# First half of x in four tile transfers, and the gates on a semaphore of their own

## The chip, the cores and the metric

The kernel runs on 1 core of a Trainium2 chip. The metric is the device time of one execution in microseconds (us); smaller is better. Its engines are TensorE (PE, with its weight loads as PEld), VectorE (DVE), ScalarE (ACT), GpSimd (POOL) and SyncE (SP), which here only issues the transfers.

## The reference, cut to what matters

x is 4 x 256 tokens of 256 channels, ctx_2048 has the same shape. Four residual steps follow each other, each gated by the tanh of one of four scalars:

```python
x = x + tanh(g_xattn[0]) * wkv(w, u, layernorm(x), ctx_2048)       # a scan over 256 tokens
x = x + tanh(g_ffn[0])   * ternary_ffn(layernorm(x), ...)          # inner size 1024
x = x + tanh(g_xattn[1]) * cross_attention(layernorm(x), ctx_2048) # 32 heads of 8
x = x + tanh(g_ffn[1])   * experts(layernorm(x), ...)              # 64 experts, top 8, and a shared one
```

In `wkv` the keys are the normed x and the values are ctx_2048; the running maximum of the keys, two decayed sums and their quotient are computed token by token in each channel.

## The kernel before

The 1024 tokens lie in x as 8 tiles of 128 tokens (TT = 8); a half is 4 tiles (HT = 4). Every engine has one stream of instructions, written out by hand, and waits on semaphores; a transfer adds 16 to its semaphore when it has landed.

SP issues all transfers. At the start it issues, with no wait between them: x, tiles 0 to 3 (`ld_x[0]`); identf, wkv, gates and identh (all on `ld_const`, which so reaches 64); ctxT (1 MB, `ld_ctx`); three blocks of FFN weights (1 MB each, `ld_ffn`); proj and gate (`ld_proj`); x, tiles 4 to 7 (`ld_x[1]`). Its first wait is for the splits of the context and the projections into halves, ahead of the expert weights.

DVE starts with `constants()`, `stats(0)` (bn_stats of tiles 0 to 3 at L1009, aggregation at L1012, then `ve`), `signs()` (the negated gates and wkv), `norm(0)` (the root's correction, then xn at L1028), `low_part(0)` (the low part of ctxT, L1287), and the scans: `running_max(0)`, `running_max(1)` (L1049, L1051), `sums_a`, `sums_b` and so on to the quotients (L1096).

ACT starts with `gains()` (tanh of the gates, L749), `table_exp_ln()` (a table load, L752), `norm_root(0)` (Ln at L564, Exp at L566), `high_context()` (the high part of ctxT, L763), `keys_before_steps(0)` (the turned keys out of PSUM, L682), `abs_sum(0)` (the first FFN block, L578), and the exponentials of the scans.

PE turns the normed tiles (L1554, `turn_norm(0)`), and next projects the context (L1562) once the projections are split.

`stats(q)` is called for 12 groups of tiles, 32 tiles in all (`NORM_TILES`); each call waits once, on the semaphore of its half:

```python
NORM_TILES = [(0, 4), (0, 4), (0, 2), (4, 8), (2, 4), (0, 2), (4, 8), (2, 4), (4, 6), (6, 8), (4, 6), (6, 8)]
```

Behind that come the FFN and attention of the first half (to about 165 us), and then 65 passes over pairs of experts (L1562 and L1892 on PE), with the second half's attention worked in among them.

Of the kernel before, what the change touches and what calls it, by code (L numbers as in the profile page):

```python
# [18 lines left out]
TT = NT // P  # L19
HT = TT // 2  # L20
# [26 lines left out]
def bass_flamingo(nc, x_in, ctxT_in, wkv_in, g_in, ffn_in, proj_in, gate_in, gu_in, dp_in,  # L47
                  identf_in, identh_in, routing, out):
    with ExitStack() as stack:
        def sb(name, shape, dt=F32):  # L50
            return stack.enter_context(nc.sbuf_tensor(name, shape, dt))

        def sem(name):
            return stack.enter_context(nc.semaphore(name))
# [4 lines left out]
        x = sb("x", [P, TT, D])  # L59
# [4 lines left out]
        gates = sb("gates", [P, 4])  # L64
# [110 lines left out]
        def bank(i, n=1):  # L175
            return ps[:, 512 * i:512 * (i + n)]


        ld_x = [sem(f"ld_x{i}") for i in range(2)]
        ld_const = sem("ld_const")  # L180
        ld_ctx = sem("ld_ctx")
        ld_proj = sem("ld_proj")
        ld_ffn = [sem(f"ld_ffn{i}") for i in range(3)]
# [85 lines left out]
        x_rows = x_in.rearrange("(t p) d -> p t d", p=P)  # L269
# [27 lines left out]
        def normed_rows(q):  # L297

            return sum(b - a for i, (a, b) in enumerate(NORM_TILES[:q]) if i not in FFN_NORMS)

        def halves_before(q):
            return DK * SPLIT_NORMS.index(q)
# [178 lines left out]

        @block.sync
        def _(sp):
            sp.dma_start(x[:, 0:HT, :], x_rows[:, 0:HT, :]).then_inc(ld_x[0], 16)
            sp.dma_start(identf[:, :], identf_in).then_inc(ld_const, 16)
            sp.dma_start(wkv[:, :, :], wkv_in).then_inc(ld_const, 16)
            sp.dma_start(gates[:, :], g_in).then_inc(ld_const, 16)
            sp.dma_start(identh[:, :], identh_in).then_inc(ld_const, 16)
            sp.dma_start(ctxT[:, :, :], ctxT_in).then_inc(ld_ctx, 16)
            for i in range(3):  # L490
                sp.dma_start(fst[i], ffn_in[:, i, :]).then_inc(ld_ffn[i], 16)
            sp.dma_start(proj[:, :, :], proj_in).then_inc(ld_proj, 16)
            sp.dma_start(gate[:, :, :], gate_in).then_inc(ld_proj, 16)
            sp.dma_start(x[:, HT:TT, :], x_rows[:, HT:TT, :]).then_inc(ld_x[1], 16)

            def load_entry(e):
                if e >= NS:
                    sp.wait_ge(mwH_ready, e - NS + 1)
                    sp.wait_ge(mwL_ready, e - NS + 1)
                p = ENTRY_PAIR[e]  # L500
                if p == SHARED:
                    to = mst[:, e % NS, 0:2 * DK * P].rearrange("p (b n) -> p b n", n=P)
                    of = gu_in[:, p, :].rearrange("p (b n) -> p b n", n=P)[:, :, 0:EI]
                    for i in range(2):
                        rows = slice(i * EI, (i + 1) * EI)
                        sp.dma_start(to[:, :, rows], of).then_inc(ld_pair[e % NS], 16)
                        sp.dma_start(mst[rows, e % NS, 2 * DK * P:PW], dp_in[0:EI, p, :]).then_inc(ld_pair[e % NS], 16)
                    return
                sp.dma_start(mst[:, e % NS, 0:2 * DK * P], gu_in[:, p, :]).then_inc(ld_pair[e % NS], 16)
                sp.dma_start(mst[:, e % NS, 2 * DK * P:PW], dp_in[:, p, :]).then_inc(ld_pair[e % NS], 16)  # L510

            def store_routing(h):
                sp.wait_ge(WT_ready, h + 1)
                sp.dma_start(routing[:, h * HALF:(h + 1) * HALF], WT[0:E + 1, :]).then_inc(WT_stored, 16)
                sp.wait_ge(WT_stored, 16 * (h + 1))

            def store_out(h):
                sp.wait_ge(out_ready, HT * (h + 1))
                sp.dma_start(out_rows[:, HT * h:HT * (h + 1), :], x[:, HT * h:HT * (h + 1), :]).then_inc(out_done, 16)


            sp.wait_ge(splitH, 3)
            sp.wait_ge(splitL, 3)
            for e in range(NS + EARLY):
                load_entry(e)
            store_routing(0)
            sp.wait_ge(y_turned, TT)
            for c in range(NCH):
                p, h = CHUNKS[c]
                if c in LOAD_IN:  # L530
                    load_entry(LOAD_IN[c])
                if c == SHARED - 1:
                    store_routing(1)
                if c == FIRST_DONE + 9:
                    store_out(0)
                if c >= NR:
                    sp.wait_ge(inter_ready, c - NR + 1)
                for i in range(2):
                    row, half = (E, i) if p == SHARED else (2 * p + i, h)
                    sp.dma_start(route[i * EI:(i + 1) * EI, c % NR, :],  # L540
                                 routing[row:row + 1, half * HALF:(half + 1) * HALF].broadcast_to([EI, HALF])
                                 ).then_inc(ld_route[c % NR], 16)
            store_out(1)
            sp.wait_ge(out_done, 32)

        @block.scalar
        def _(act):
# [197 lines left out]
                                     scale=ROUTING_SCALE).then_inc(WT_ready, 1)  # L745

            def gains():
                act.wait_ge(ld_const, 64)
                nc.scalar.activation(tg[:, :], gates[:, :], ACT.Tanh).then_inc(tanh_done, 1)  # L749

            def table_exp_ln():
# [13 lines left out]
            def high_projections():  # L765
                act.wait_ge(ld_proj, 32)
                nc.scalar.activation(projH[:, :, :], proj[:, :, :], ACT.Copy, scale=W_SCALE).then_inc(splitH, 1)
                nc.scalar.activation(gateH[:, :, :], gate[:, :, :], ACT.Copy, scale=W_SCALE).then_inc(splitH, 1)

            gains()  # L770
            table_exp_ln()
            norm_root(0)
# [184 lines left out]
        def _(dve):  # L957
            done = [0]

            def post(ins):  # L960
                done[0] += 1
                ins.then_inc(v_ord, 1)

            def settle():
                dve.wait_ge(v_ord, done[0])
# [8 lines left out]
            def root_begin(src, n, mul, eps):  # L974
                e = begun[0]
                begun[0] += 1
                V.tensor_scalar(ve[:, e % 2, 0:n], src, mul, eps, ALU.mult, ALU.add).then_inc(var_ready, 1)
# [26 lines left out]
            def stats(q):  # L1004

                a, b = NORM_TILES[q]
                dve.wait_ge(ld_x[a // HT], 16)
                for t in range(a, b):
                    post(V.bn_stats(bn[:, t, :], x[:, t, :]))  # L1009
                settle()  # L1010
                for t in range(a, b):
                    post(V.bn_aggr(mv[:, t, :], bn[:, t, :]))  # L1012
                settle()
                if q < BITS_FROM:
                    root_begin(mv[:, a:b, 1], b - a, 1.0, LN_EPS)
# [286 lines left out]
            def signs():  # L1302
                dve.wait_ge(tanh_done, 1)
                post(V.tensor_scalar(ntg[:, :], tg[:, :], -1.0, None, ALU.mult))
                post(V.tensor_scalar(tgd[:, :], tg[:, 3:4], DOWN_UNSCALE, None, ALU.mult))
                dve.wait_ge(ld_const, 64)
                V.tensor_scalar(nwkv[:, :, :], wkv[:, :, :], -1.0, None, ALU.mult).then_inc(wkv_negated, 1)

            constants()
            stats(0)  # L1310
            signs()
            norm(0)
# [14 lines left out]
            row_sums(0)  # L1327
            add_y(0, 4)
            stats(1)
            ternary_weights(0)  # L1330
            norm(1)
# [8 lines left out]
            ffn_residual(1, 6)  # L1340
            row_sums(1)
            stats(2)
            rows_begin(0)
            norm(2)
# [181 lines left out]
        def _(pe):  # L1526
# [3 lines left out]
            def take(b, sem_value):  # L1530

                if b in reader:
                    pe.wait_ge(*reader[b])
                reader[b] = sem_value

            def turn_norm(q, b0):

                a, b = NORM_TILES[q]
                if q == 0:
                    pe.wait_ge(ld_const, 64)  # L1540
                for k in range(DK):
                    if q in FFN_NORMS:
                        take(b0 + k, (xq_ready, DK * FFN_NORMS.index(q) + k + 1))
                    elif q in STEP_NORMS:
                        take(b0 + k, (kT_ready, DK * STEP_NORMS.index(q) + k + 1))
                    else:
                        take(b0 + k, (hL_ready, halves_before(q) + k + 1))
                for t in range(a, b):
                    if q in FFN_NORMS:
                        pe.wait_ge(xz_ready, t + 1)  # L1550
                    else:
                        pe.wait_ge(xn_ready, normed_rows(q) + t - a + 1)
                    for k in range(DK):
                        mm = T.transpose(bank(b0 + k)[:, (t - a) * P:(t - a + 1) * P], xn[:, t, k * P:(k + 1) * P], identf[:, :])  # L1554
                mm.then_inc(xn_turned, 1)
# [419 lines left out]
```

## Time and profile before

| | before |
|---|---|
| runs | 495.12, 496.13, 498.81 us; median 496.13 |
| profiled execution, its own time | 494.66 us |
| its span | 492.9 us |
| busy PE, DVE, ACT | 401.6 (81%), 384.4 (78%), 305.9 us (62%) |
| mean granted TensorE clock | 0.946 of full speed |
| DMA | 47.47 MB, mean 96 GB/s |

The span is the profiler's, from the first instruction to the last; the device time of the same execution is 1.76 us longer. A busy share is an average over stages with different limits, so that the place of the change, the first 13 us, has to be read from views of that stretch. "SPq" is the issue of a transfer on SP; the data moves later, by the DMA engines.

### The profile page before, as it was taken

The page shows a single profiled execution, that of the slowest core. Times are in us where ns is not written, and L with a number is a line of the kernel's source. Part 1 is how long each engine was busy: PE and PEld are TensorE (multiplying, and loading weights), DVE is VectorE, ACT ScalarE, POOL GpSimd, SP SyncE. Part 2 cuts the span into 40 slices and gives each one's busy share as a digit, 9 for nine tenths or more (in the row PEclk, how much of TensorE's full clock was granted, in tenths as well). Part 3 has the DMA queues.
Part 4 walks back from the last instruction along what each step waited for, and adds up shares of the span by engine and source line. Part 5 has one row for each costly group of instructions (what it writes and reads, how often), then busy time and mean ns, then how long its engine had stood idle before and what let it go on. Part 6 is the DMA issues. An engine that isn't in the chain of part 4 may idle for free.

```text
span 492.9 us, 7899 instructions
## 1 busy us (share of the span) xinstructions
PE 401.6 (81%) x2606; PEld 191.7 (39%) x2606; DVE 384.4 (78%) x867; ACT 305.9 (62%) x473; POOL 0.2 (0%) x4
## 2 busy tenths in 40 slices
PE   1041765777774999989999899899999999999994
PEld 1020353332332555444334433444444444444442
DVE  5999489898999789999878876886546776677744
ACT  5989576689893785648887678463233445544431
POOL 0000000000000000000000000000000000000000
PEclk9996889595998799999999999999999999999999
DMA  8420000000020151525246332234421755555501
GB/s 306 198 65 1 0 1 1 1 1 2 1 65 4 47 165 57 158 88 168 67 118 191 98 108 72 91 108 125 132 65 54 217 164 164 164 177 172 171 22 43
DMA packets 31491, 47.47 MB, mean 96 GB/s; under 512 B 5594, under 2 KB 15194, under 8 KB 30940
## 3 DMA queue, kind: packets, MB, share of 16 engines
q1 hardware_dynamic: 31452, 46.98, 30.4%
q8 instruction: 21, 0.34, 0.3%
q14 instruction: 18, 0.15, 0.1%
HBM read 45.65 MB, written 1.31 MB: 95 GB/s over the span
## 4 chain that ended last, share of the span: by engine, by line
PE 47%; DVE 30%; ACT 8%; issue 7%; DMA 5%; SPq 2%; DVEq 0%; ACTq 0%
PE ps L1562 25%; PE ps L1892 12%; PE ps L1667 4%; DMA regP<-in_dp_dram 4%; PE ps L1655 2%; DVE regW L1277 2%; DVE bn L1009 1%; DVE tiny L1194 1%; ACT regO L584 1%; DVE xn L1028 1%; DVE regW L1481 1%; DVE regW L1472 1%; PE ps L1583 1%; DVE rep L1155 1%; DMA regC<-in_ctxT_dram 1%
## 5 line engine op out<-in xcount | busy, mean ns | idle before, releaser
L1562 PE MATMUL ps<-hH,regC 128*128 128x512 f16 x264 | 85.5, 379 | 1.1 <-ACT regW L934 0.9
L1481 DVE TENSOR_TENSOR regW<-ps,regW 128x512 f32<-128x512 f32 x65 | 44.9, 690 | 52.6 <-PE ps L1562 50.1
L934 ACT ACTIVATE regW<-ps 128x512 f32<-128x512 f32 x52 | 31.0, 596 | 86.6 <-PE ps L1562 83.5
L1562 PE MATMUL ps<-hH,regW 128*128 128x512 f16 x248 | 81.8, 386 | 1.4 <-ACT regW L934 0.8
L1562 PE MATMUL ps<-hL,regC 128*128 128x512 f16 x132 | 50.0, 379 | 0.0
L1892 PE MATMUL ps<-regW,regC 128*128 128x512 f16 x198 | 48.2, 379 | 0.5 <-DVE regW L1472 0.5
L1562 PE MATMUL ps<-hL,regW 128*128 128x512 f16 x124 | 47.8, 385 | 0.0
L1892 PE MATMUL ps<-regW 128*128 128x512 f16 x186 | 45.3, 380 | 0.7 <-DVE regW L1472 0.7
L1472 DVE TENSOR_TENSOR regW<-regW 128x512 f16<-128x512 f32 x65 | 44.4, 682 | 1.0 <-ACT regW L941 0.7
L941 ACT CAST regW<-regW 128x512 f16<-128x512 f32 x65 | 39.8, 612 | 6.4 <-DVE regW L1494 6.1
L1562 PEld LDWEIGHTS ps<-hH,regC 128*128 128x128 f16 x264 | 25.8, 98 | 33.3 <-issue 2.6
L723 ACT ACTIVATE exs<-ps 128x1024 f32<-128x1024 f32 x32 | 32.0, 1023 | 9.4 <-PE ps L1655 8.6
L1562 PEld LDWEIGHTS ps<-hH,regW 128*128 128x128 f16 x248 | 24.5, 99 | 33.0 <-issue 3.9
L1494 DVE TENSOR_TENSOR regW<-regW 128x512 f32<-128x512 f32 x52 | 35.6, 685 | 0.1
L723 ACT ACTIVATE regF<-ps 128x1024 f32<-128x1024 f32 x32 | 32.0, 1026 | 5.0 <-PE ps L1667 2.2
L732 ACT ACTIVATE regC<-regP 128x768 f16<-128x768 f32 x30 | 25.3, 844 | 15.7 <-DMA regP<-in_dp_dram 15.7
L1277 DVE SCALAR_TENSOR_TENSOR regC<-regP,regC 128x768 f16<-128x768 f32 x30 | 28.5, 953 | 8.1 <-ACT regC L732 8.0
L1554 PE MATMUL ps<-identf,xn 128*128 128x128 f32 x64 | 12.6, 341 | 26.4 <-DVE xn L1028 15.8
L1655 PE MATMUL ps<-regO,KT 32*128 32x256 f16 x256 | 21.8, 290 | 9.4 <-ACT exs L723 3.8
L1892 PEld LDWEIGHTS ps<-regW,regC 128*128 128x128 f16 x198 | 19.1, 98 | 24.1 <-DVE regW L1472 1.0
L732 ACT ACTIVATE regW<-regP 128x768 f16<-128x768 f32 x27 | 22.6, 844 | 8.8 <-DMA regP<-in_dp_dram 8.5
L1277 DVE SCALAR_TENSOR_TENSOR regW<-regP,regW 128x768 f16<-128x768 f32 x27 | 25.5, 952 | 2.9 <-ACT regW L732 2.9
(189 smaller groups left out, 657.1 us busy)
## 6 DMA issues: line engine op xcount, KB each, us to landing
regW<-routing_dram SPq DMA_DIRECT2D x130, 128.0 KB, 3.1
regP<-in_gu_dram SPq DMA_DIRECT2D x56, 256.0 KB, 2.7
regP<-in_dp_dram SPq DMA_DIRECT2D x56, 128.0 KB, 2.8
regO<-in_ffn_dram SPq DMA_DIRECT2D x3, 1024.0 KB, 9.0
x<-in_x_dram SPq DMA_DIRECT2D x2, 512.0 KB, 8.2
regC<-in_ctxT_dram SPq DMA_DIRECT2D x1, 1024.0 KB, 5.0
out_dram<-x SPq DMA_DIRECT2D x2, 512.0 KB, 3.3
regP<-in_proj_dram SPq DMA_DIRECT2D x1, 768.0 KB, 12.1
```

What stands on the lines that cost most here:

```text
L723: nc.scalar.activation(Ex[u % NE], bank(b0, 2).rearrange("p (j n) -> p j n", j=2), ACT.Exp, scale=float(HD) ** -0.5).then_inc(prob_ready, 1)
L732: nc.scalar.activation(mwH[e % NW], mst[:, e % NS, :], ACT.Copy, scale=W_SCALE).then_inc(mwH_ready, 1)
L934: nc.scalar.activation(sgm[:, c % 2, :], bank(gate_bank(c)), ACT.Silu, scale=UNSCALE).then_inc(esilu_done, 1)
L941: nc.scalar.copy(inH[:, d % 2, :], inter[:, d % 2, :]).then_inc(inH_ready, 1)
L1277: V.scalar_tensor_tensor(mwL[e % NW], mst[:, e % NS, :], W_SCALE, mwH[e % NW], ALU.mult, ALU.subtract).then_inc(mwL_ready, 1)
L1472: V.tensor_tensor(inL[:, d % 2, :], inter[:, d % 2, :], inH[:, d % 2, :], ALU.subtract).then_inc(inL_ready, 1)
L1481: V.tensor_tensor(rows, bank(gate_bank(c) + 1), rows, ALU.mult).then_inc(et_done, 1)
L1494: V.tensor_tensor(rows, route[:, c % NR, :], sgm[:, c % 2, :], ALU.mult).then_inc(inter_ready, 1)
L1562: mm = T.matmul(out_ap, w(k), a(k), start=(n == 0), stop=(n == 3 * DK - 1))
L1655: mm = T.matmul(bank(b0 + jj)[:, mt * S:(mt + 1) * S], KT[r:r + 32, g, b * S + mt * P:b * S + (mt + 1) * P], QT[r:r + 32, g, (b % 2) * S:( ...
L1667: mm = T.matmul(bank(bk)[32 * j:32 * j + HD + 1, 0:S], vaug[:, 2 * b + mt, 4 * g + j, :], Ex[u % NE][:, j % 2, mt * S:(mt + 1) * S], start ...
L1892: mm = T.matmul(bank(ACC[h] + k), w[s][:, at], a[:, c % 2, :], start=(c == 0 and n == 0), stop=(c == NCH - 1 and n == 2), skip_group_check ...
```

## The change

The first half of x is loaded by four transfers of one tile each, each on a semaphore of its own; the second half takes the fifth. The gates are loaded between the first and the second tile, on `ld_gates`. ScalarE's tanh waits for `ld_gates` alone; the others wait for the three transfers left on `ld_const` (48 in place of 64). DVE's `stats` waits ahead of each tile, not once ahead of a group.

```diff
-        ld_x = [sem(f"ld_x{i}") for i in range(2)]
+        ld_x = [sem(f"ld_x{i}") for i in range(HT + 1)]
         ld_const = sem("ld_const")
+        ld_gates = sem("ld_gates")
@@ SP
-            sp.dma_start(x[:, 0:HT, :], x_rows[:, 0:HT, :]).then_inc(ld_x[0], 16)
+            for t in range(HT):
+                sp.dma_start(x[:, t, :], x_rows[:, t, :]).then_inc(ld_x[t], 16)
+                if t == 0:
+                    sp.dma_start(gates[:, :], g_in).then_inc(ld_gates, 16)
             sp.dma_start(identf[:, :], identf_in).then_inc(ld_const, 16)
             sp.dma_start(wkv[:, :, :], wkv_in).then_inc(ld_const, 16)
-            sp.dma_start(gates[:, :], g_in).then_inc(ld_const, 16)
             sp.dma_start(identh[:, :], identh_in).then_inc(ld_const, 16)
             sp.dma_start(ctxT[:, :, :], ctxT_in).then_inc(ld_ctx, 16)
@@
-            sp.dma_start(x[:, HT:TT, :], x_rows[:, HT:TT, :]).then_inc(ld_x[1], 16)
+            sp.dma_start(x[:, HT:TT, :], x_rows[:, HT:TT, :]).then_inc(ld_x[HT], 16)
@@ ACT gains()
-                act.wait_ge(ld_const, 64)
+                act.wait_ge(ld_gates, 16)
                 nc.scalar.activation(tg[:, :], gates[:, :], ACT.Tanh).then_inc(tanh_done, 1)
@@ DVE stats(q)
-                dve.wait_ge(ld_x[a // HT], 16)
                 for t in range(a, b):
+                    dve.wait_ge(ld_x[min(t, HT)], 16)
                     post(V.bn_stats(bn[:, t, :], x[:, t, :]))
@@ DVE signs()
-                dve.wait_ge(ld_const, 64)
+                dve.wait_ge(ld_const, 48)
@@ PE turn_norm(0)
-                    pe.wait_ge(ld_const, 64)
+                    pe.wait_ge(ld_const, 48)
```

## Rows read from the trace of the kernel before

**Rows 1.** The page's chain that ended last, its shares by engine.
```profile
PE 47%; DVE 30%; ACT 8%; issue 7%; DMA 5%; SPq 2%; DVEq 0%; ACTq 0%
```

**Rows 2.** That chain in order of time, 0 to 40 us: start, length, what.
```profile
3.18 4.96 DMA regC<-in_ctxT_dram
...
10.22 0.05 issue
```

**Rows 3.** Timeline of ACT, 0 to 16 us: start, length, operation, idle before and its releaser.
```profile
5.12 0.21 ACT L749 ACTIVATE tg<-gates 128x4 f32<-128x4 f32 x1 [3.12 <-DMA identh<-in_identh_dram]
5.35 1.28 ACT L752 ACT_TABLE_LOAD   x1
6.64 0.20 ACT L564 ACTIVATE lnv<-ve 128x4 f32<-128x4 f32 x1
...
8.25 1.91 ACT L763 ACTIVATE ctxH<-regC 128x2048 f16<-128x2048 f32 x1 [1.17 <-DMA regC<-in_ctxT_dram]
10.52 1.07 ACT L682 COPY regC<-ps 128x512 f32<-128x512 f32 x2 [0.36 <-PE ps L1554]
11.48 1.92 ACT L578 ACTIVATE regF<-regO 128x2048 f32<-128x2048 f32 x1
```

**Rows 4.** Timeline of DVE, 0 to 40 us.
```profile
4.32 1.41 DVE L1009 BATCH_NORM_STATS2 bn<-x 128x6 f32<-128x256 f32 x4 [2.58 <-DMA x<-in_x_dram]
...
6.18 0.17 DVE L977 TENSOR_SCALAR ve<-mv 128x4 f32<-128x4 f32 x1
...
7.99 1.38 DVE L1028 TENSOR_SCALAR xn<-x,mv,rstd 128x256 f32<-128x256 f32 x4
10.27 2.29 DVE L1287 SCALAR_TENSOR_TENSOR ctxL<-regC,ctxH 128x2048 f16<-128x2048 f32 x1 [0.90 <-ACT ctxH L763]
12.48 1.27 DVE L1049 TENSOR_TENSOR_SCAN regW<-wkv,regC 128x256 f32<-128x256 f32 x2
...
36.73 1.66 DVE L1178 SCALAR_TENSOR_TENSOR x<-ps,ntg,x 128x256 f32<-128x256 f32 x4
```

**Rows 5.** Timeline of SP's queue, 0 to 8 us: start and length of each issue.
```profile
0.73 0.43 SPq L484 DMA_DIRECT2D x<-in_x_dram  x1
1.22 0.49 SPq L485 DMA_DIRECT2D identf<-in_identf_dram  x1
...
2.23 0.43 SPq L487 DMA_DIRECT2D gates<-in_g_dram  x1
2.70 0.43 SPq L488 DMA_DIRECT2D identh<-in_identh_dram  x1
3.18 0.43 SPq L489 DMA_DIRECT2D regC<-in_ctxT_dram  x1
```

**Rows 6.** Stretches of 0.25 us: clock, DMA share and GB/s stand last.
```profile
4.40:4.65 0.25, 0.00 (x0) 0.00 (x0) 0.25 (x1) 0.00 (x0) 0.00 (x0) 1.00 0.00 0
...
5.40:5.65 0.25, 0.00 (x0) 0.00 (x0) 0.25 (x2) 0.25 (x1) 0.00 (x0) 1.00 1.09 459
```

**Rows 7.** DMA issues of 0 to 40 us: count, KB each, median us to landing.
```profile
identf<-in_identf_dram SPq DMA_DIRECT2D x1, 64.0 KB, 3.1
identh<-in_identh_dram SPq DMA_DIRECT2D x1, 32.0 KB, 2.4
...
gates<-in_g_dram SPq DMA_DIRECT2D x1, 2.0 KB, 2.5
```

**Rows 8.** Line L484 alone: time from issue to landing.
```profile
DMA to landing us min/median/max: 3.6/3.6/3.6
```

**Rows 9.** Line L491 alone, the three FFN blocks.
```profile
DMA to landing us min/median/max: 7.0/9.0/11.0
```

**Rows 10.** Line L1178 alone: durations of one in ns.
```profile
L1178 DVE SCALAR_TENSOR_TENSOR x<-ps,ntg,x x8: 474/476/485, 36.7 to 131.8; 128x256 f32<-128x256 f32 x8
```

**Rows 11.** Longer stretches: length, busy PE, PEld, DVE, ACT, POOL, granted clock, DMA.
```profile
82.60:96.30 13.70, 8.42 (x69) 4.58 (x70) 12.72 (x37) 7.52 (x13) 0.00 (x0) 0.57 0.01 1
...
110.00:120.10 10.10, 5.75 (x52) 1.60 (x56) 9.50 (x21) 9.66 (x18) 0.00 (x0) 0.60 0.00 1
120.20:154.20 34.00, 23.70 (x292) 12.52 (x284) 31.83 (x92) 26.48 (x40) 0.00 (x0) 0.97 0.08 25
...
164.50:488.70 324.20, 313.50 (x1860) 144.64 (x1858) 242.64 (x498) 184.07 (x284) 0.00 (x0) 1.00 0.39 119
```

## The prediction

> **What bounds the kernel now.** I read the page's chain first. It ends on PE (47%) and passes through DVE (30%) [rows 1], and from 164.5 to 488.7 us PE is busy 313.50 of 324.20 us at the full granted clock [rows 11]: the passes over the experts are bound by PE. The change doesn't touch that part; it can only make it begin sooner or later. So the question is what sets the start of the work, and the chain in order of time answers it: at the front of the chain stands not x, but the load of ctxT, issued at 3.18 us and landed 4.96 us later, at 8.14 [rows 2]. I then read each engine's timeline over the first 16 us, to see both paths that meet at the first scan.
>
> The path of x: the first half lands 3.6 us after its issue at 0.73 [rows 5, 8], bn_stats starts at 4.32 and `ve` at 6.18 [rows 4]. ACT has its tanh only at 5.12, after 3.12 us of idleness that identh's landing ended, and the table load behind it runs from 5.35 to 6.63; so Ln starts at 6.64, 0.29 us after `ve` is finished at 6.35 [rows 3, 4]. The normed tiles start at 7.99 and are done at 9.37 [rows 4].
>
> The path of ctxT: ACT is idle 1.17 us until it lands, makes ctxH from 8.25 to 10.16, and DVE, idle for 0.90 us, makes ctxL from 10.27 to 12.56; the first scan starts at 12.48 [rows 3, 4]. In DVE's stream ctxL stands ahead of the scan, and in ACT's stream ctxH stands ahead of the copy of the keys. The copy runs from 10.52 to 11.59 [rows 3], so the keys are there 0.89 us before DVE is free to scan. Of the two paths the one of ctxT ends last, twice: once at ACT (the idle 1.17 us) and once at DVE (the idle 0.90 us). What the change hastens is the other one.
>
> **Part by part.**
>
> *The three additional transfers.* SP issues five transfers ahead of ctxT, at 0.73, 1.22, ... and 2.70, and ctxT itself at 3.18: (3.18 - 0.73) / 5 = 0.49 us from one to the next [rows 5]. With the change eight stand ahead of it: four of x, gates, identf, wkv, identh. It is issued 3 x 0.49 = 1.47 us later, at 4.65. What lies beside this: nothing on SP, whose queue has no wait here.
>
> Does a later issue make a later landing? Only if the DMA engines aren't still busy with what lies ahead. From 4.40 to 4.65 us they moved nothing at all, 0 GB/s, and from 5.40 they move 459 GB/s [rows 6]. The queues had run dry before ctxT's data began, so its landing follows from its issue. I take the whole 1.47 us: landing at 4.65 + 4.96 = 9.61. The bounds are 0, if ctxT's own transfer goes faster in its new place, and 3 x (2.23 - 1.22) / 2 = 1.52 us at the widest spacing shown [rows 5]; a case below 0 is excluded, since no transfer is taken from in front of ctxT.
>
> *The Trainium skill on this cost.* The rows put 0.43 us of SP's time and 0.49 us of spacing on one issue. "DMA: Bandwidth & Descriptors", section "Anatomy of one DMA — SWDGE (gpsimd) path", puts about 50 ns on the sequencer's dispatch and calls descriptor generation small. By that page three more issues would be an estimated 0.15 us, and the sum would be 0.15 in place of 1.47. The page describes transfers issued by GpSimd and these are SP's; this trace doesn't agree with the page's figure.
>
> *The tiles of x.* Their issues come at 0.73, 1.70, 2.19 and 2.68 us (gates at 1.22). No load of 128 KB stands alone at the start; a 64 KB one landed 3.1 us after its issue, a 32 KB one 2.4 and a 2 KB one 2.5 [rows 7], and four tiles at once took 3.6 [rows 8]. So a tile takes between 2.4 and 3.6; I take 2.6, near the small ones, as its data is a quarter of x's. Tile 0 is there at about 3.3 and tile 3 at 5.3 (5.1 to 6.3). Before, all four were there at about 4.3. Three of the bn_stats run earlier under the loads, the fourth starts at about 5.3 and is done at 5.7, which is where the last of the four ended before, 4.32 + 1.41 = 5.73 [rows 4]. So the stats of the half gain nothing: `ve` stays at about 6.2, with 6.0 to 7.1 as its bounds.
>
> *The gates.* They land at 1.22 + 2.5 = 3.7 [rows 7]; tanh and its following table load are done at about 3.7 + 0.05 + 0.21 + 0.02 + 1.28 = 5.3, in place of 6.63 [rows 3]. Then Ln waits for `ve` alone and starts at about 6.4, a gain of 0.25 us. The xn tiles end at about 9.1 in place of 9.37. All of this ends at ACT's wait for ctxT, which now lasts until 9.61: worth nothing.
>
> *identf, wkv and identh.* identf and wkv move back by four places (1.96 us), identh by three (1.47 us), since gates used to stand between wkv and identh. identh, the last of the three, is issued at 4.17 and lands 2.4 us later [rows 7], at about 6.6. DVE's `signs()` waits for it, and queued behind that wait are `norm(0)` and all that follows; but `norm(0)` needs ACT's root, which comes at about 6.9. The cover is 0.3 us. PE waits for the same semaphore, and needs xn until about 7.7 anyway. If identh is late by more than the cover, the xn path moves, and it has room: xn may end 1 us late before the copy of the keys waits.
>
> *What is then late next.* ctxH runs from 9.72 to 11.63, ctxL from 11.74 to 14.03, and the first scan starts at about 13.95 in place of 12.48. The copy of the keys stands behind ctxH in ACT's stream; before, it waited 0.36 us for PE's last turn [rows 3], now PE has long finished, and it runs from about 11.65 to 12.75, still ahead of the scan. Then the first FFN block: it lands 7.0 us after its issue at the soonest of the three [rows 9], about 10.7 before and 12.1 after, and `abs_sum(0)` took it at 11.48 [rows 3] and will at 12.65. Cover 0.5 us, and behind it another idle stretch until the first exponential. The other blocks, proj, gate and the second half of x have many microseconds.
>
> *The additional waits in stats.* 12 waits become 32, 20 more. Whether a wait for a semaphore long reached costs DVE anything, I read from the residual sum at L1178, which also waits ahead of each tile: four took 1.66 us [rows 4] and one 0.476 [rows 10], so that (1.66 - 0.476) / 3 = 0.395 us lie between starts, less than one lasts. The wait is hidden behind the running instruction. Bounds: 0 and 20 x 0.05 = 1.0 us, with 0.05 as a typical gap of the chain [rows 2]; I take 0.
>
> *How far the shift gets.* From the first scan on DVE, ACT and PE hand work to each other, and no transfer of the start is awaited that has less than the cover named above. A uniform shift of all three engines then reaches the expert passes whole, and the end with them. The one thing tied to time and activity rather than to semaphores is TensorE's clock. In 82.6 to 96.3 and in 110.0 to 120.1 us the granted clock averaged 0.57 and 0.60 [rows 11], nearly at the 1.2 GHz level of its two. If the edges of these stretches move against the work, the sum changes by a share of a microsecond per edge.
>
> **The sum.** +1.47 (ctxT's issue), 0 (stats), 0 (tanh), 0 (waits) = +1.47 us. Against the profiled execution's own time this is 494.66 + 1.5 = 496.1. That execution was 1.5 us below the median of the runs, so on the median it is 496.13 + 1.47 = 497.6 us, 0.3% slower. No change of this kernel under 1% can be told from none by its measurement, whose three runs span 0.7%.
>
> **The rivals.**
>
> *The landing doesn't follow the issue, or slack swallows the shift (not slower).* If what sets ctxT's landing is the bytes queued ahead of it, which the change leaves equal, it lands at 8.14 still. For it: the DMA engines run near full share from 5.4 us. Against it: the stretch with 0 GB/s just before [rows 6]. Or the first scan has slack further on. Then the xn path, 0.25 us earlier, still ends behind ctxH, and the time is 496.1 us, at best 0.25 less.
>
> *The clock turns against it (slower).* If moving the work by 1.5 us puts one more stretch of 10.2 us at half clock into 120 to 154 us, where PE is busy 23.70 of 34.00 us [rows 11], up to 0.70 x 10.2 / 2 = 3.6 us are lost: 497.6 + 3.6 = 501.2. It decides from the point where PE is on the chain in that stretch. For it: such stretches exist on both sides of it. Against it: the pattern of work is the same, only moved.
>
> *The clock turns in its favour.* One such stretch less, of 110.0 to 120.1, with 5.75 us of PE, gives back at most 2.9 us [rows 11]: 494.7.
>
> *The additional waits cost what they can.* 497.6 + 1.0 = 498.6.
>
> **How the numbers follow.** The forecast has 0.60 (496.9 to 498.2), no shift 0.15, the clock against it 0.10, half of it over the 1% bound, the clock in its favour 0.08, the waits 0.07. The predicted time is 497.6. The range goes down to 495.0, past no shift at all and into the favourable clock, and up to 500.3, past the waits and into the unfavourable clock. Over 1% faster would take a second stretch of clock in its favour, 0.03; over 1% slower 0.05; within 1% 0.92.
>
> **What would show it.** SP's queue: ctxT issued at 4.65. ACT: tanh at about 3.8, then Ln at 6.4, then an idle time of about 2.7 us ended by ctxT's landing. DVE: the last bn_stats at 5.3, ctxL at 11.7, the first scan at 13.9. The expert passes begin 1.5 us later. I am wrong if ctxT lands as early as before, if the first scan starts before 13, or if the delay at 13 us is no longer there at 165.

## The result, and the profile after

| | before | changed |
|---|---|---|
| median of 20 runs | 495.54 us | 498.23 us |
| lowest, highest | 494.04, 498.81 | 495.50, 500.99 |
| profiled execution, its own time | 494.66 | 499.49 |
| its span | 492.9 | 497.6 |

The ratio is 1.0038 with a 95% interval from 1.0021 to 1.0055: slower by 1.9 us (1.0 to 2.7), below the 1% that counts as no change. 1.47 us had been forecast, and 498.23 lies inside the range of 495.0 to 500.3.

The timeline of SP's queue in the changed kernel (start, length, what was issued):

```profile
0.73 0.38 SPq L486 DMA_DIRECT2D x<-in_x_dram  x1
1.17 0.42 SPq L488 DMA_DIRECT2D gates<-in_g_dram  x1
1.64 1.38 SPq L486 DMA_DIRECT2D x<-in_x_dram  x3
3.06 0.43 SPq L489 DMA_DIRECT2D identf<-in_identf_dram  x1
...
4.48 0.43 SPq L492 DMA_DIRECT2D regC<-in_ctxT_dram  x1
```

It answers to [rows 5]. ctxT is issued at 4.48 in place of 3.18, 1.30 us later for three issues more. 1.47 had been worked out from 0.49 us an issue; here the eight ahead of ctxT follow each other by 0.47 us on average, (4.48 - 0.73) / 8. ACT's timeline, to be held against [rows 3]:

```profile
3.04 0.20 ACT L752 ACTIVATE tg<-gates 128x4 f32<-128x4 f32 x1 [1.04 <-DMA gates<-in_g_dram]
3.27 1.28 ACT L755 ACT_TABLE_LOAD   x1
6.08 0.20 ACT L567 ACTIVATE lnv<-ve 128x4 f32<-128x4 f32 x1 [1.52 <-DVE ve L980]
...
9.61 1.91 ACT L766 ACTIVATE ctxH<-regC 128x2048 f16<-128x2048 f32 x1 [3.10 <-DMA regC<-in_ctxT_dram]
11.43 1.05 ACT L685 COPY regC<-ps 128x512 f32<-128x512 f32 x2
```

The reader should see two things. What the change set out to hasten is earlier: tanh at 3.04 and not 5.12, Ln at 6.08 and not 6.64. And all of it ends in an idle time that grew from 1.17 to 3.10 us: ACT stands and waits for ctxT. DVE shows the same, to be held against [rows 4]:

```profile
2.88 0.43 DVE L1012 BATCH_NORM_STATS2 bn<-x 128x6 f32<-128x256 f32 x1 [1.14 <-DMA x<-in_x_dram]
4.09 1.33 DVE L1012 BATCH_NORM_STATS2 bn<-x 128x6 f32<-128x256 f32 x3 [0.79 <-DMA x<-in_x_dram]
...
7.42 1.38 DVE L1031 TENSOR_SCALAR xn<-x,mv,rstd 128x256 f32<-128x256 f32 x4
11.63 2.29 DVE L1290 SCALAR_TENSOR_TENSOR ctxL<-regC,ctxH 128x2048 f16<-128x2048 f32 x1 [2.83 <-ACT ctxH L766]
13.84 1.27 DVE L1052 TENSOR_TENSOR_SCAN regW<-wkv,regC 128x256 f32<-128x256 f32 x2
```

The normed tiles start 0.57 us earlier (7.42 for 7.99), ctxL and the first scan 1.36 us later (13.84 for 12.48). The two profiled executions, however, differ by 4.8 us, not 1.4. The rest comes behind the scans. The chain in order of time, changed kernel first, then the kernel before (start, length, what):

```profile
30.12 1.77 DVE projL L1290
...
31.93 5.28 PE ps L1565 x12
37.24 0.38 ACT kc L632
```

```profile
35.22 0.69 DVE regC L1096
...
36.35 6.06 ACT regO L584 x3
```

In the changed kernel's execution the 12 matmuls of the first projections are themselves on the chain; in the one of before they were not. So one of the experiments, e9, is the question how far two executions of the same program differ.

### The profile page after: what moved, and what is told of

The parts are those of the page before. It is cut to its first block, busy times and chain, and to the rows that moved or that the text cites. A ratio compares the mean times of both kernels' runs of the same rounds, so it can differ in the third digit from the quotient of the medians.

```text
span 497.6 us, 7902 instructions
## 1 busy us (share of the span) xinstructions
PE 404.6 (81%) x2606; PEld 193.4 (39%) x2606; DVE 384.9 (77%) x867; ACT 305.9 (61%) x473; POOL 0.2 (0%) x4
## 4 chain that ended last, share of the span: by engine, by line
PE 49%; DVE 30%; ACT 7%; issue 7%; DMA 4%; SPq 2%; DVEq 0%; ACTq 0%
PE ps L1565 26%; PE ps L1895 12%; PE ps L1670 4%; DMA regP<-in_dp_dram 3%; DVE tiny L1197 2%; PE ps L1658 2%; DVE regW L1280 2%; DVE bn L1012 2%; DVE xn L1031 1%; ACT regO L587 1%; DVE regW L1484 1%; DVE regW L1475 1%; DVE regF L1209 1%; PE ps L1586 1%; DMA regC<-in_ctxT_dram 1%
```

## The experiments

My theory: ctxT's landing sets the first scan, it follows from its issue, each issue ahead of it costs 0.47 to 0.49 us, and the shift reaches the end whole; split, waits and gates cost and give nothing. Rivals: the split of x or the 20 waits cost by themselves; slack swallows the shift; the landing goes by the bytes ahead; the difference is the clock's. Every ratio is to runs of the kernel before on the same chip. The columns "x through" and "ctxT begins" come from the list of packets in the trace: x's first half travels in 512 packets of 1 KB, ctxT and the FFN blocks in packets of 8 KB. They give the end of x's last packet and the start of the first 8 KB packet; "to landing" is the time from ctxT's issue to its landing.

| kernel | ctxT issued | x through | ctxT begins | to landing | first scan | ratio, 95% interval |
|---|---|---|---|---|---|---|
| before | 3.18 | 3.87 | 4.23 | 5.0 | 12.48 |  |
| e9, before again | 3.19 | 3.84 | 4.26 | 5.5 | 12.99 | 1.0019 (0.9998 to 1.0040) |
| changed | 4.48 | 4.64 | 5.55 | 5.0 | 13.84 | 1.0038 (1.0021 to 1.0055) |
| e11, changed again | 4.48 | 4.49 | 5.55 | 5.1 | 13.89 | 1.0039 (1.0015 to 1.0063) |
| e1, three issues more | 4.61 | 3.70 | 5.68 | 5.3 | 14.23 | 1.0011 (0.9991 to 1.0032) |
| e4, nine issues more | 7.46 | 3.69 | 8.53 | 5.0 | 16.75 | 1.0087 (1.0061 to 1.0114) |
| e5, waits alone | 3.19 | 3.75 | 4.25 | 5.3 | 12.82 | 1.0013 (0.9988 to 1.0038) |
| e6, gates alone | 3.19 | 3.80 | 4.27 | 5.6 | 13.17 | 1.0019 (0.9991 to 1.0046) |
| e2, ctxT sixth, small ones behind | 3.06 | 4.68 | 4.15 | 7.0 | 15.04 | 1.0015 (0.9996 to 1.0034) |
| e3, ctxT third, small ones behind | 1.77 | 3.93 | 3.77 | 7.6 | 14.40 | 1.0019 (0.9998 to 1.0039) |
| e7, small ones by ACT, ctxT third | 1.78 | 4.90 | 3.98 | 7.3 | 13.38 | 1.0012 (0.9985 to 1.0039) |
| e8, small ones by ACT, ctxT sixth | 3.06 | 5.07 | 4.42 | 7.5 | 14.94 | 1.0053 (1.0028 to 1.0077) |
| e10, identh last | 2.72 | 3.76 | 3.85 | 5.6 | 12.65 | 0.9977 (0.9952 to 1.0002) |
| e12, identh last, gates second | 2.71 | 3.88 | 4.41 | 5.4 | 12.50 | 1.0006 (0.9979 to 1.0033) |

**e1, e4: the issues without the split.** The kernel before with 3 or 9 transfers of 2 KB into a spare tile ahead of ctxT:

```diff
             sp.dma_start(identh[:, :], identh_in).then_inc(ld_const, 16)
+            for i in range(3):      # 9 in e4
+                sp.dma_start(spare[:, i, :], g_in).then_inc(ld_spare, 16)
             sp.dma_start(ctxT[:, :, :], ctxT_in).then_inc(ld_ctx, 16)
```

> The kernel before with three additional 2 KB transfers between identh and ctxT; x whole, the gates and all waits as they were. If the cost of the change is the three additional issues ahead of ctxT: ctxT issued at about 4.5 to 4.6 us, landed at about 9.5, first scan at about 13.8, time 1.4 us above before plus whatever the clock does (ratio 1.003, within 1.001 to 1.0055). If the cost lies in the split of x or in the additional waits on DVE: first scan at 13.8 all the same, but a time equal to before (ratio 1.000), or the landing stays at 8.1 if only bytes count.

> As the first of these, with nine additional 2 KB transfers: the suspected cost three times over. If a shift of the first scan reaches the end whole: ctxT issued at 3.2 + 9 x 0.47 = 7.4, first scan at 16.7, time 4.2 us above before (ratio 1.0085, 1.006 to 1.011). If the difference of the change is the clock's (more half-clock stretches after any disturbance of the start, whatever its size): ratio 1.003 to 1.005 here as well. If slack swallows a part: under 1.006.

SP's queue in e4, then DVE's timeline in e4:

```profile
3.19 4.23 SPq L492 DMA_DIRECT2D spare<-in_g_dram  x9
7.46 0.43 SPq L493 DMA_DIRECT2D regC<-in_ctxT_dram  x1
```

```profile
16.75 1.27 DVE L1054 TENSOR_TENSOR_SCAN regW<-wkv,regC 128x256 f32<-128x256 f32 x2
```

Nine issues take 4.23 us, 0.47 each; ctxT lands 5.0 us after its issue, and the scan is 4.27 us late. The time, from six runs, is 0.87% longer, 4.3 us (3.0 to 5.7). Within that interval the shift reaches the end whole, and it isn't a fixed toll of the clock. e1 repeats the changed kernel's place of ctxT (issued at 4.61) with x in one piece and moves the scan by 1.75 us; its ratio of 1.0011 holds 0 as well as 1.6 us and decides nothing on the time.

**e5, e6: the other parts alone.** e5 has only the waits ahead of each tile, e6 only the gates, second in the queue with their own semaphore; the tanh waits for that one, and the other waits on `ld_const` go from 64 to 48.

```diff
-                dve.wait_ge(ld_x[a // HT], 16)
                 for t in range(a, b):
+                    dve.wait_ge(ld_x[t // HT], 16)      # e5
```

```diff
             sp.dma_start(x[:, 0:HT, :], x_rows[:, 0:HT, :]).then_inc(ld_x[0], 16)
+            sp.dma_start(gates[:, :], g_in).then_inc(ld_gates, 16)      # e6; removed from ld_const
```

> The kernel before with nothing but the waits of the change: stats waits ahead of each tile, on the semaphore of its half, 20 waits more. If satisfied waits are free: every group of four bn_stats lasts 1.41 us as before, first scan at 12.5, ratio 1.000 (0.998 to 1.002). If each costs a gap of 0.05 us on the path: groups of 1.56 us, 1.0 us more in all, ratio 1.002.

> The kernel before with nothing but the gates' part of the change: second in the queue and on a semaphore of their own; x in one transfer, ctxT sixth as before. If only ctxT's landing counts: tanh about 0.5 to 1 us earlier, Ln at 6.4, ctxT landed at 8.1 and scan at 12.5, ratio 1.000. If the tanh and its table load were on the path: scan at 12.2, ratio 0.9995; the time can't tell these two apart, the trace can.

The second group of bn_stats in e5, all of whose waits are long satisfied (DVE's timeline):

```profile
38.76 1.41 DVE L1009 BATCH_NORM_STATS2 bn<-x 128x6 f32<-128x256 f32 x4
```

1.41 us for four, as without the waits [rows 4]. The satisfied waits cost nothing here. ACT's timeline of e6:

```profile
4.48 0.20 ACT L750 ACTIVATE tg<-gates 128x4 f32<-128x4 f32 x1 [2.47 <-DMA gates<-in_g_dram]
...
6.35 0.20 ACT L565 ACTIVATE lnv<-ve 128x4 f32<-128x4 f32 x1 [0.37 <-DVE ve L978]
...
8.94 1.91 ACT L764 ACTIVATE ctxH<-regC 128x2048 f16<-128x2048 f32 x1 [2.15 <-DMA regC<-in_ctxT_dram]
```

The tanh is 0.64 us earlier, Ln 0.29, and ACT then waits 2.15 us for ctxT: worth nothing, as with the tiles. ctxT itself landed 5.6 us after its issue at 3.19, where I had expected 5.0.

**e2, e3: giving ctxT its place back, or a better one.** e2 is the changed kernel, e3 the kernel before with the gates second; in both, identf, wkv and identh move behind ctxT.

```diff
+            sp.dma_start(ctxT[:, :, :], ctxT_in).then_inc(ld_ctx, 16)
             sp.dma_start(identf[:, :], identf_in).then_inc(ld_const, 16)
             sp.dma_start(wkv[:, :, :], wkv_in).then_inc(ld_const, 16)
             sp.dma_start(identh[:, :], identh_in).then_inc(ld_const, 16)
-            sp.dma_start(ctxT[:, :, :], ctxT_in).then_inc(ld_ctx, 16)
```

> The changed kernel with ctxT moved ahead of identf, wkv and identh, so that it is the sixth issue as before the change; four tile transfers, gates on their own semaphore and all waits kept. If only ctxT's issue counts: issued at about 3.1, landed at 8.1, ctxH at 8.2, scan at 12.4 to 12.5, ratio to before 1.000 (0.999 to 1.001). Rival: identf and identh now land behind 1 MB of context, near 8.2 or later, DVE's wait for identh holds norm(0) back and the normed path takes over as the last; the scan then comes at 12.5 to 13.5 and up to 1 us of the cost stays. If the split or the waits cost by themselves, the ratio stays at 1.003 with the scan at 12.5.

> The kernel before with x in one transfer, then the gates (own semaphore), then ctxT third, then identf, wkv, identh. If issue order sets the start: ctxT issued at 1.7 instead of 3.2, but its data now stands directly behind the 512 KB of x, so landing at about 6.7; ctxH at about 7.0, and DVE's norm(0), which waits for identh behind 1 MB of context until about 7, becomes the last: xn 8 to 9.4, ctxL from 9.4, scan at 11.6. Time 0.8 us below before (ratio 0.9985, 0.997 to 1.000). If the start is not on the path of the end, ratio 1.000.

Both missed. The landings (DMA issues of the first 15 us: count, KB, us to landing) and DVE's timeline of e3:

```profile
regC<-in_ctxT_dram SPq DMA_DIRECT2D x1, 1024.0 KB, 7.6
...
identf<-in_identf_dram SPq DMA_DIRECT2D x1, 64.0 KB, 5.6
identh<-in_identh_dram SPq DMA_DIRECT2D x1, 32.0 KB, 6.8
```

```profile
10.02 0.17 DVE L1308 TENSOR_SCALAR nwkv<-wkv 128x4 f32<-128x4 f32 x1 [3.53 <-DMA identh<-in_identh_dram]
...
12.20 2.28 DVE L1288 SCALAR_TENSOR_TENSOR ctxL<-regC,ctxH 128x2048 f16<-128x2048 f32 x1
...
14.40 1.27 DVE L1050 TENSOR_TENSOR_SCAN regW<-wkv,regC 128x256 f32<-128x256 f32 x2
```

ctxT, issued 1.41 us earlier than before, landed 1.2 us later, after 7.6 us in place of 5.0. And identh landed at 10, so that DVE, which waits for it ahead of `norm(0)`, lost the normed path too (3.53 us idle): ctxL starts at 12.20 with no idle time before it, behind the normed tiles. So here the normed path comes last, and in e2 as well (ctxL at 12.84, with no idle time before it either). It is the rival that e2's expectation names, with a larger effect than it allowed. These two kernels therefore don't isolate the split of x, as I had meant them to.

**e7, e8: the small ones out of SP's queue.** ScalarE issues identf, wkv and identh before its first table load; e8 is otherwise the changed kernel, e7 the kernel of e6.

```diff
+            for to, of in ((identf[:, :], identf_in), (wkv[:, :, :], wkv_in), (identh[:, :], identh_in)):
+                act.dma_start(to, of).then_inc(ld_const, 16)
             gains()
```

> As the one before, and identf, wkv and identh are issued by ScalarE's queue, so that SP issues x, gates, ctxT and then the FFN blocks. ctxT is issued at 1.7. If ctxT's landing follows its issue with 5.0 us wherever large blocks stand behind it: landed at about 6.8, scan limited by the normed path and ctxL behind it, at 11.5 to 11.8, time 0.8 us below before (ratio 0.9985). If small transfers in flight beside a large one stretch it, whichever queue they come from (as when they stood behind it on SP's queue, 7.0 and 7.6 us instead of 5.0): landed at 9 or later, scan at 13.5 or later, ratio over 1.002.

> The changed kernel, four tiles and gates first, with identf, wkv and identh issued by ScalarE's queue, so that ctxT is SP's sixth issue as before the change. If the cost of the change is ctxT's place alone: ctxT issued at 3.1, landed at 8.1, scan at 12.4, ratio 1.000. If the split of x costs by itself: ratio 1.003 with that scan. If small transfers beside it stretch it: landing at 9 or later.

Landing of ctxT in e8, and e8's stretches from the start of ctxT's data to its landing (length, busy times, clock, DMA share, GB/s):

```profile
regC<-in_ctxT_dram SPq DMA_DIRECT2D x1, 1024.0 KB, 7.5
...
identh<-in_identh_dram ACTq DMA_DIRECT2D x1, 32.0 KB, 3.2
```

```profile
4.40:10.50 6.10, 1.94 (x8) 1.57 (x8) 3.93 (x19) 1.00 (x3) 0.00 (x0) 1.00 0.96 341
```

and the kernel before over the corresponding stretch:

```profile
4.40:8.10 3.70, 0.00 (x0) 0.00 (x0) 2.85 (x17) 1.90 (x4) 0.00 (x0) 1.00 0.86 341
```

Small loads in flight beside ctxT can't be the cause in e8: there they have landed at 1.65 + 3.2 = 4.85 us, when ctxT's data has hardly begun. The rate is the same 341 GB/s. But in e8 6.10 x 341 = 2.08 MB passed before ctxT (1.05 MB) was complete, 1.98 MB of them in 8 KB packets, in the kernel before 3.70 x 341 = 1.26 MB. So about 0.7 MB more of the FFN blocks, which were issued later, had moved ahead of ctxT's last part. In e2 and e3 it is another picture: 269 GB/s from 4.20 to 10.10 us and 294 GB/s from 3.80 to 9.40 us, 1.6 MB each, with the packets of identf, wkv and identh among them. e8 is the slowest of the kernels with ctxT in sixth place, with the scan at 14.94 and a ratio of 1.0053: the landing counts, not the issue. e7 landed at 9.1 and its scan came at 13.38, near the second branch of what was expected; its ratio of 1.0012 was under it.

What the four slow landings have in common stands in the table. In the ten executions with 5.0 to 5.6 us x is through before ctxT begins, by 0.09 us (e10) to 4.84 us (e4). In the four with 7.0 to 7.6 us ctxT begins while packets of x are still under way, by 0.16 us (e3) to 0.92 us (e7). This is a regularity in 14 traces, not a shown cause: no experiment changed it alone, and all four also have small loads behind ctxT or on ScalarE's queue.

**e9, e11: the same two kernels again.** No edit.

> The kernel before, unchanged, as a control for the small ratios. Ratio 1.000 (0.998 to 1.002). Its profile is a second look at the start of that kernel: if the start of the first look was typical, ctxT lands at 8.1 to 8.5 and the first scan starts at 12.5 to 12.9. The places of the half-clock stretches should differ between the two looks although the program is the same.

> The changed kernel again, on the same chip as the control. If its cost is ctxT's place in the queue alone: scan at 13.8, ratio 1.003 (1.001 to 1.005), of which 1.36 us is the shift seen at the scan. If there is more to it than the shift: ratio 1.004 or more while the control stays at 1.000.

The chain of e9, in order of time:

```profile
29.26 1.77 DVE projL L1287
31.07 5.31 PE ps L1562 x12
36.41 0.39 ACT kc L629
```

In the second look at the kernel before, ctxT took 5.5 us, the scan began at 12.99, and the 12 matmuls took 5.31 us and stood on the chain, as in the changed kernel. Its own time was 497.53 us, 2.9 us above the first look. So of the 4.8 us between the first two profiles at most 1.4 are seen at the scan, and executions of one program differ by nearly as much as the rest (2.9 of 3.4). Taken together, the four looks put the scan at 12.5 and 13.0 before, 13.8 and 13.9 after: 1.1 us. The medians of the two on the same chip are 497.19 and 498.28, also 1.1 us, but the other 29 runs of the kernel before on that chip have 495.78. The control's own ratio of 1.0019 says how little a ratio under 1.002 means here.

Is the delay still there when the expert passes begin? The first matmul of the passes, in the kernel before, e9, the changed kernel and e11:

```profile
162.34 0.62 PE L1562 MATMUL ps<-hH,regW 128*128 128x512 f16 x1
```

```profile
165.66 0.62 PE L1562 MATMUL ps<-hH,regW 128*128 128x512 f16 x1
```

```profile
166.50 0.62 PE L1565 MATMUL ps<-hH,regW 128*128 128x512 f16 x1
```

```profile
165.07 0.62 PE L1565 MATMUL ps<-hH,regW 128*128 128x512 f16 x1
```

Two executions of the program before lie 3.32 us apart, more than the shift. One reason is in the stretches in which the granted clock is at half. From 153.20 to 155.60 us, in the same order (length, busy times, clock, DMA share, GB/s):

```profile
153.20:155.60 2.40, 0.78 (x4) 0.32 (x4) 2.26 (x7) 0.00 (x0) 0.00 (x0) 1.00 0.00 0
```

```profile
153.20:155.60 2.40, 2.40 (x13) 2.40 (x12) 1.47 (x5) 0.58 (x2) 0.00 (x0) 0.50 0.02 7
```

```profile
153.20:155.60 2.40, 2.04 (x10) 2.08 (x11) 1.54 (x5) 1.41 (x3) 0.00 (x0) 0.50 0.00 0
```

```profile
153.20:155.60 2.40, 2.40 (x20) 1.86 (x18) 2.29 (x6) 0.86 (x2) 0.00 (x0) 1.00 0.03 7
```

So I compare only executions whose stretches at full and at half clock, by the trace's records of the granted clock, have the same order and lengths up to the passes:

| pair | apart at the first scan | apart at the passes |
|---|---|---|
| e9, changed | 0.85 us | 0.84 us |
| e5, e11 | 1.07 | 1.26 |
| e12, e4 | 4.25 | 4.32 |
| e5, e2 | 2.22 | 2.11 |
| e5, e3 | 1.58 | 1.81 |
| e9, e8 | 1.95 | 1.50 |
| e9, e6 | 0.18 | -0.07 |
| e9, e10 | -0.34 | -0.87 |

The shift arrives at the passes to within 0.3 us in six of the eight pairs and 0.6 us in all. The first pair also bears on the split of x and the waits: between the scan and the passes they add nothing that these two executions show.

**e10, e12: one issue less ahead of ctxT.** identh is first used at 76.9 us; it is issued last, with a semaphore of its own that PE waits for at its first use. e12 has the gates second as well.

```diff
-            sp.dma_start(identh[:, :], identh_in).then_inc(ld_const, 16)
@@
             sp.dma_start(x[:, HT:TT, :], x_rows[:, HT:TT, :]).then_inc(ld_x[1], 16)
+            sp.dma_start(identh[:, :], identh_in).then_inc(ld_half, 16)
```

> The kernel before with identh issued last, behind the second half of x, on its own semaphore; so four transfers stand ahead of ctxT instead of five. If one issue less is worth one issue: ctxT issued at 2.7, landed at 7.7 with 5.0 us, ctxH at 7.8, first scan at 12.0, 0.47 us below before (ratio 0.999). If ctxT's time to landing grows whenever it is issued sooner after x (5.6 to 7.6 us in the kernels where less or other work stood ahead of it), it lands at 8.5 or later and the ratio is 1.000 to 1.002.

> The kernel before with the gates second in the queue on a semaphore of their own (the half of the change that adds no issue) and identh issued last: x, gates, identf, wkv, ctxT, FFN blocks, proj, gate, x's second half, identh. If one issue less ahead of ctxT is worth 0.47 us and the earlier tanh frees the normed path: ctxT issued at 2.7, landed at 8.2 with the 5.5 us of the second look at the kernel before, scan at 12.5, 0.3 to 0.5 us below the control, ratio 0.998 to 1.000. If the start with identh last gained by chance: ratio 1.000 to 1.002, as the control has it.

ctxT is issued at 2.72 and 2.71, the scan comes at 12.65 and 12.50. ACT's timeline of e12 shows that ACT still waits for ctxT:

```profile
8.27 1.91 ACT L765 ACTIVATE ctxH<-regC 128x2048 f16<-128x2048 f32 x1 [1.43 <-DMA regC<-in_ctxT_dram]
```

Neither branch of e10's expectation was met: ctxT landed 5.6 us after its issue, at 8.3. With the 5.4 to 5.6 us of this pair the scan is 0.3 to 0.5 us before the control, which took 5.5. The times say 0.9977 (0.9952 to 1.0002) and 1.0006 (0.9979 to 1.0033). Neither is shown to beat the kernel before. e10 had the lowest median of all, 495.01, but e12, with an earlier scan, doesn't repeat it.

## Why the prediction was right

The time moved the way that was forecast, and the cause is the one named: three issues more ahead of the load that is awaited last.

*The bound.* ctxT's landing stood last at ACT and DVE, as read. The changed kernel's idle time of 3.10 us at ctxH (2.7 forecast) shows it once more.

*ctxT's issue, the one term of the sum.* 1.47 forecast, 1.30 measured: the issues follow each other by 0.44 to 0.48 us in the changed kernel, not 0.49. With the landing at 5.0 us, as assumed, the scan came at 13.84 (13.95 forecast). The assumption behind it, that the landing follows the issue, held for additional small issues ahead of ctxT (e1: 5.3, e4: 5.0), and failed in e2, e3, e7 and e8 (7.0 to 7.6 us). The prediction has the condition for it, that the DMA engines aren't still busy with what lies ahead, and read it from a wrong row: a stretch counts the packets that begin in it, so that 0 GB/s from 4.40 to 4.65 us doesn't mean idle engines. The stretch before it in the same view shows it:

```profile
4.15:4.40 0.25, 0.00 (x0) 0.00 (x0) 0.08 (x1) 0.00 (x0) 0.00 (x0) 1.00 2.42 327
```

ctxT's first packets had begun from 4.23 on and were under way. The conclusion stood all the same, since x was through at 3.87; that the wrong row led to the right answer is luck. e2, e3 and e7 were reckoned with the same 5.0 us, and missed; in all three, and in e8, x wasn't through.

*The bounds of that term* rested on one look at the kernel before, whose 5.0 us to landing was the shortest of the three that had its order (5.0, 5.3 in e5, 5.5 in e9). Against the mean of those scans, 12.8, the change costs 1.1 us. *The absolute time* stood on the median of three runs, 496.13; over 20 it is 495.54. Between the medians of 20 lie 2.7 us, not 1.47, so that 497.6 for a measured 498.23 is closer than the forecast of the difference was.

*The tiles.* I took 2.6 us to landing and a gain of 0. They landed in 2.1 to 2.4, the last stats ended at 5.42 and not 5.73, a gain of 0.3 us. *The gates* landed in 1.9, not 2.5, the tanh came at 3.04, not 3.8. Both terms were off, without effect, since they are hidden.

*The waits.* 0, confirmed by e5: 1.41 us per group.

*The shift reaches the end.* "I am wrong if the delay at 13 us is no longer there at 165": between the first two profiles it is 4.16 us there, between e9 and e11 -0.59, and between e9 and the changed kernel, whose clock stretches agree, 0.84 of 0.85. So it is there, though two single profiles with different clock stretches can hide it. At the end e4's 4.27 us at the scan give 4.3 (3.0 to 5.7). Not every kernel agrees: e2's scan lies 2.3 us behind the mean scan of 12.8, and its time is 0.7 us longer with an interval that ends at 1.7, although its trace has the delay at the passes (2.11 us behind e5). Over the 13 kernels of the table that have a ratio, a straight line through ratio x 496 us against the scan's start rises 0.87 us per us, with a correlation of 0.80; without e4 it rises 0.63, with 0.58. That the shift arrives whole is thus shown up to 165 us, and at the end only by e4. Whether the 0.8 us between the change's 1.9 and the 1.1 of the scans is more than scatter stays open: its interval, 1.0 to 2.7, holds both. The split of x was never run alone with ctxT landing as before, so a cost of its own behind 165 us isn't excluded by an experiment.

*The Trainium skill on an issue.* The estimate from the page "DMA: Bandwidth & Descriptors", section "Anatomy of one DMA — SWDGE (gpsimd) path", 0.15 us for three, is not borne out for SP's issues: nine in e4 took 4.23 us of SP's time.

*The clock* was a rival in both directions. The medians don't need it, but the half-clock stretches are one part of what separates single executions, as the four rows at 153 us show.

## What to carry to other kernels

At the start of a kernel the issuing queue is a resource like an engine: each transfer takes 0.38 to 0.49 us of it here, and splitting one load to hasten its first consumer delays every load behind it. Before such a split, look for the load that is awaited last; if it stands behind the one to be split, the split costs its number of additional issues, however early the first consumer starts. To move that load forward isn't a sure gain either: in all four kernels in which it began before x was through it landed 2 us later than otherwise. And a profile of one execution carries its own luck: two looks at the same program differed by 2.9 us, more than the effect in question, so that the place of the shift has to be read at a point shortly behind the change, or between executions with the same clock stretches, and the size from many runs.

## What the runs showed of the hardware

Landing of a 1 MB load is not its issue plus a constant. It took 5.0 to 5.6 us in the ten executions in which the load ahead of it was through when its first packet began, and 7.0 to 7.6 in the four in which it wasn't; in e8 at the same rate, with 2.08 MB in place of 1.26 MB moved meanwhile.

The first matmuls behind a long idle time run at half rate, for a length that differs between executions of one program. PE's timeline in the changed kernel, behind 22 us of idleness, and e11's:

```profile
31.93 0.61 PE L1565 MATMUL ps<-projH,ctxH 128*128 128x512 f16 x1 [22.01 <-DVE projL L1290]
32.34 0.63 PE L1565 MATMUL ps<-projL,ctxH 128*128 128x512 f16 x1
...
36.60 0.60 PE L1565 MATMUL ps<-projH,ctxL 128*128 128x512 f16 x1
```

```profile
35.80 0.59 PE L1565 MATMUL ps<-projH,ctxH 128*128 128x512 f16 x1
36.22 0.38 PE L1565 MATMUL ps<-projL,ctxH 128*128 128x512 f16 x1
36.44 0.38 PE L1565 MATMUL ps<-projH,ctxL 128*128 128x512 f16 x1
```

Starts lie 0.43 us apart throughout the first, and 0.22 us apart once e11's became fast. Matmuls of the same size lie 0.41 to 0.43 us apart where the clock is granted at half, 1.2 GHz, as at the start of the passes in the kernel before:

```profile
162.40:164.40 2.00, 2.00 (x8) 0.66 (x6) 1.77 (x14) 0.94 (x4) 0.00 (x0) 0.50 0.00 0
```

The views print a clock of 1.00 at 32 us too, but that isn't a measurement: the trace's records of the granted clock begin only at 33.45 us in the kernel before, 36.21 in e11 and 37.04 in the changed kernel, each time where the matmuls become fast or the twelve are over, and a view takes a stretch without a record for 1.00. So the spacing, and not the printed clock, tells the rate there.

In the first look at the kernel before, 7 matmuls were slow and 5 fast, and the chain went past them over DVE; in e9, the same program, all 12 were slow and on the chain, and ScalarE's next work started at 37.49 and not 36.35 us. That is 1.1 us between two executions of one program, 0.5 of it already there at the scan.
